# Decoder layer on one core: the result rows of the expert stage are stored by GpSimd, one indexed scatter per batch, in place of one plain transfer per four batches from SyncE

## The chip, the cores and the metric

The kernel runs on one core of a Trainium2 chip. The metric is device time in microseconds (us), the median of the timed runs. The engines are named as in the profile: PE (TensorE), PEld (its weight loads), DVE (VectorE), ACT (ScalarE), POOL (GpSimd) and SP (SyncE); SPq is SP's queue, from which it issues DMAs.

## The reference

Input x has 64 batches of 128 tokens, 128 wide; ctx has 64 batches of 120. Three blocks follow each other, each ending in a layer norm over the sum with its input:

```
x = layernorm(x + linear_attention(x))                  # 16 heads of 8, softplus q and k, causal
x = layernorm(x + cross_attention(ctx, x))              # 16 heads of 64; queries from x, keys from ctx and x
x = layernorm(x + experts(x))                           # the output
```

The last block, in which the change lies:

```
scores  = softmax(x @ gate_w.T)                         # 8 experts
top 2 of them, weights normalised and times 2.5 -> combine[token, expert]
y       = sum_e combine[:, e] * (silu(x @ w_gate[e]) * (x @ w_up[e])) @ w_down[e]     # width 176 each
y      += silu(x @ sw_gate) * (x @ sw_up) @ sw_down     # shared expert, width 352
out     = (h - mean(h)) / sqrt(var(h) + 1e-5),  h = x + y
```

All of it is float32. The kernel gets float32 products from three passes of TensorE over operands split into a high and a low part.

## The kernel before

The three blocks run one after the other: `linear_attention`, `cross_attention` and `experts`. X, the layer's current value, stays in on-chip memory; token s of every batch lies on partition s. The order of the work on each engine is written out by hand: there is one instruction stream per engine, and semaphores tie the streams together.

`experts` works on groups of four batches, 512 tokens at once: 16 groups. The hidden width of the eight experts and the shared one, 1408 + 352 = 1760, is cut into 14 blocks of 128 (the last has 96); blocks 0 to 10 belong to the experts, 11 to 13 to the shared one. Step t of the pipeline works on three groups at once: it prepares group t (transposes, logits, routing), runs the 14 blocks of group t-1, and finishes group t-2 (normalises and stores).

In block n of a step:
- PE multiplies by gate and up, three matmuls each (`split_product`, L489 to L491), spreads the routing weights for an expert block (L1325), and adds block n-3 into `ps_y` (the down product), for which it waits until `hidden_lo` of that block is there. At the start of the next step it transposes the routing weights `c_rows` (L1347).
- ACT takes SiLU (L1172) and rounds the previous block's `hidden` to `hidden_hi` (L1161).
- DVE multiplies SiLU by up (L1257) and, for an expert block, by the routing weight (L1263). From block 8 on it also runs a share of the 20 small routing operations of group t (L1217 to L1240), the last four in block 13, behind that block's L1257. Its write of `hidden` in block n waits until POOL has finished `hidden_lo` of block n-2, since `hidden` has two buffers.
- POOL computes `hidden_lo = hidden - hidden_hi` of block n-1 (L1117, function `hidden_lo`). In block 4 it makes the reciprocal deviation of group t-2 (L1131, L1133); in blocks 5, 7, 9 and 11 it writes one batch's normalised rows into `result` (L1138), each behind that block's `hidden_lo`.
- SP waits for the four `result` rows of group t-2 and issues one 256 KB store (L1098). `result` has two buffers, `par` 0 and 1, and `stored[par]` counts landed stores.

At the start of `experts` POOL writes three constants (L1107 to L1110): `half`, the expert numbers `index`, for which DVE waits before it copies the first `x_rows`, and the zeroed `cT`.

Of the kernel before, what the change touches and what calls it, by code (L numbers as in the profile page):

```python
# [24 lines left out]
P = 128  # L25
EXPERTS = 8
B = 64
S = 128
# [6 lines left out]
def wait(engine, semaphore, count):  # L35

    if not isinstance(count, int) or count > 0:
        engine.wait_ge(semaphore, count)  # L38


def wait_apart(engine, opened, *waits):

    waits = [(semaphore, count if isinstance(count, int) else engine.to_reg(count)) for semaphore, count in waits]
    engine.wait_ge(opened, 1)
    for semaphore, count in waits:
        wait(engine, semaphore, count)


def pipelined(engine, step, count=B, head=4, tail=4):

    for t in range(count + tail):
        step(t, t % 2)


def there(s, count=B):

    return not isinstance(s, int) or 0 <= s < count


def landed(s, parity):

    return (s - parity) * 8 + 16
# [943 lines left out]
GROUP = 4  # L1010
TOKENS = GROUP * S
GROUPS = B // GROUP
# [3 lines left out]
def experts(nc, X, ident, later, out):  # L1016
# [19 lines left out]
    with ExitStack() as stack:  # L1036
        room = Room(nc, stack, "e")
# [24 lines left out]
        result = room.sbuf("result", [P, 2, GROUP, D])  # L1062
# [7 lines left out]
        half_ready = room.sem("half_ready")  # L1070
# [10 lines left out]
        sum_ready, stat_ready, mom_ready = room.sem("sum_ready"), room.sem("stat_ready"), room.sem("mom_ready")  # L1081
        vare_ready, rstd_ready, result_ready = room.sem("vare_ready"), room.sem("rstd_ready"), room.sem("result_ready")
        stored = [room.sem(f"stored{n}") for n in range(2)]
        block = stack.enter_context(nc.Block())

        def run(engine, step):
            pipelined(engine, step, GROUPS, 2, 2)

        def here(s):
            return there(s, GROUPS)  # L1090

        @block.sync
        def _(sp):
            def step(t, par):
                s2 = t - 2
                if here(s2):
                    sp.wait_ge(result_ready, (s2 + 1) * GROUP)
                    sp.dma_start(out[bass.ds(s2 * GROUP, GROUP)].rearrange("b s d -> s b d"), result[:, par]  # L1098
                                 ).then_inc(stored[par], 16)

            run(sp, step)
            for par in range(2):
                sp.wait_ge(stored[par], GROUPS // 2 * 16)

        @block.gpsimd
        def _(pool):
            nc.gpsimd.memset(half[:], -0.5).then_inc(half_ready, 1)  # L1107
            for e in range(EXPERTS):
                nc.gpsimd.memset(index[:, e:e + 1], float(e)).then_inc(index_ready, 1)
            nc.gpsimd.memset(cT[:].bitcast(F32), 0.0).then_inc(zero_ready, 1)  # L1110
            pool.wait_ge(half_ready, 1)

            def hidden_lo(s, n):

                rows = rows_of[n]
                pool.wait_ge(hidden_hi_ready, s * NB + n + 1)
                nc.gpsimd.tensor_tensor(hidden_part[1][0:rows, n % RING, :], hidden[0:rows, n % 2, :],  # L1117
                                        hidden_part[0][0:rows, n % RING, :].bitcast(F32), ALU.subtract
                                        ).then_inc(hidden_lo_ready, 1)

            def step(t, par):
                s1, s2 = t - 1, t - 2
                for n in range(NB):
                    if n == 0 and here(s2):
                        hidden_lo(s2, NB - 1)
                    if n and here(s1):
                        hidden_lo(s1, n - 1)
                    if n == 4 and here(s2):

                        wait_apart(pool, half_ready, (mom_ready, (s2 + 1) * GROUP))  # L1130
                        nc.gpsimd.tensor_scalar(vare[:], mom[:, :, 1], EPS, None, ALU.add).then_inc(vare_ready, 1)  # L1131
                        pool.wait_ge(vare_ready, s2 + 1)
                        nc.gpsimd.tensor_tensor(rstd[:], vare[:], half[:], ALU.pow).then_inc(rstd_ready, 1)  # L1133
                    if n in (5, 7, 9, 11) and here(s2):
                        k = (n - 5) // 2

                        wait_apart(pool, half_ready, (rstd_ready, s2 + 1), (stored[par], landed(s2, par) - 16))
                        nc.gpsimd.tensor_scalar(result[:, par, k, :], hsum[:, k, :], mom[:, k, 0:1], rstd[:, k:k + 1],  # L1138
                                                ALU.subtract, ALU.mult).then_inc(result_ready, 1)

            run(pool, step)

        @block.scalar
# [239 lines left out]
def decoder(nc, x, ctx, Wq, bq, Wk, bk, Wv, bv, Wo, bo, m_g, m_b, l_g, l_b, xWq, xWkv, xWout,  # L1383
            gate_w, w_gate, w_up, w_down, sw_gate, sw_up, sw_down, out):
    lat = nc.dram_tensor("latents", (B, S, D), F32, kind="Internal").ap()
    with ExitStack() as stack:
        X = stack.enter_context(nc.sbuf_tensor("X", [P, B * D], F32))
        ident = stack.enter_context(nc.sbuf_tensor("ident", [P, P], F32))
        tri = stack.enter_context(nc.sbuf_tensor("tri", [P, P], F32))
        later = LaterWeights(nc, stack, (m_g, m_b, l_g, l_b), xWq, xWkv, xWout, gate_w, w_gate, w_up, w_down, sw_gate,  # L1390
                             sw_up, sw_down)
        constants(nc, ident, tri)
        linear_attention(nc, X, lat, ident, tri, x, (Wq, Wk, Wv, Wo), (bq, bk, bv, bo), later)
        cross_attention(nc, X, lat, ctx, ident, later)
        experts(nc, X, ident, later, out)
# [23 lines left out]
```

## Time and profile before

| | us |
|---|---|
| median of 3 runs | 2271.53 (2271.13 to 2274.04) |
| the profiled execution, its own time | 2267.62 |
| its span, first to last instruction | 2265.6 |
| granted TensorE clock, mean over the span | 0.985 of full speed |
| busy: PE, DVE, ACT, POOL | 2163.8, 1575.9, 1479.8, 1386.0 |

The span is that of one execution; it was taken 3.9 us under the median of the timed runs. `experts` fills it from 1697 us on. Each instruction has a line of the kernel, an engine and the names of the tiles it writes and reads; `out<-in` is the order. In brackets behind an instruction stands how long its engine had been idle and who ended that. The DMAs of the result appear as instructions of SPq, with the issue's own duration and, apart from it, the time to landing.

### The profile page before, as it was taken

Reading aid. Unit: us, or ns where it says so; the run is one execution under the profiler, and the core shown is the slowest. Engines: PE = TensorE matmul, PEld = TensorE weight load, DVE = VectorE, ACT = ScalarE, POOL = GpSimd, SP = SyncE. Lnnn points to the kernel's source line nnn. Section 1 sums busy time; section 2 is a strip of 40 time slices with the busy share of each in tenths; the row PEclk is TensorE's granted clock in tenths of the full one; section 3 lists DMA queues with packets and bytes.
Section 4 is the critical chain, followed back from the end, with each engine's and each line's share of the span. In section 5 each row is a group of like instructions: output and inputs, shape, how many; then the busy total and the mean of one; then the engine's idle time right before and its main releaser. Section 6 shows DMA issues by size and latency. Waiting matters only on the chain. (4 is left out here: it accounts for less than half of the span.)

```text
span 2265.6 us, 44642 instructions
## 1 busy us (share of the span) xinstructions
PE 2163.8 (96%) x16233; PEld 1841.5 (81%) x16233; DVE 1575.9 (70%) x3455; ACT 1479.8 (65%) x3820; POOL 1386.0 (61%) x1481
## 2 busy tenths in 40 slices
PE   6899967999999999999999999999989999999998
PEld 3455547999999999999999999999977777777776
DVE  3899965666666666666666666666657777777775
ACT  4788845667676666666676766666655665665664
POOL 4788856566565565565665655655654666666666
PEclk9999979999999999999999999999999999999999
DMA  3311110000000000000000000000000000000000
GB/s 93 113 33 33 30 30 5 6 10 6 10 7 6 10 6 6 11 6 6 11 6 10 7 6 10 6 6 10 6 1 1 10 5 10 10 5 10 10 5 14
DMA packets 52794, 33.46 MB, mean 15 GB/s; under 512 B 2968, under 2 KB 50274, under 8 KB 52450
## 3 DMA queue, kind: packets, MB, share of 16 engines
q1 hardware_dynamic: 50174, 26.30, 4.0%
q10 hardware_dynamic: 2404, 4.33, 0.7%
q8 instruction: 131, 2.15, 0.4%
q14 instruction: 85, 0.70, 0.1%
HBM read 22.22 MB, written 8.39 MB: 14 GB/s over the span
## 5 line engine op out<-in xcount | busy, mean ns | idle before, releaser
L653 POOL TENSOR_TENSOR x_prob<-x_prob,x_inv 128x496 f32<-128x496 f32 x514 | 521.7, 1015 | 546.9 <-DVE x_inv L792 546.9
L728 ACT ACTIVATE x_prob<-x_ps_S,x_nmax 128x248 f32<-128x248 f32 x1028 | 473.2, 468 | 130.4 <-DVE x_nmax L786 130.3
L786 DVE TENSOR_REDUCE x_nmax<-x_ps_S 128x2 f32<-128x496 f32 x515 | 345.5, 671 | 181.3 <-PE x_ps_S L491 181.1
L736 ACT COPY x_probT<-x_ps_T 124x512 f32<-124x512 f32 x512 | 300.7, 587 | 225.0 <-PE x_ps_T L955 225.0
L1117 POOL TENSOR_TENSOR e_hidden_lo<-e_hidden,e_hidden_hi 128x512 fp32r<-128x512 f32 x224 | 291.8, 1306 | 196.6 <-ACT e_hidden_hi L1161 195.7
L489 PE MATMUL x_ps_S<-x_kT_lo,x_G_hi 128*128 128x248 f32 x1030 | 329.6, 320 | 0.0
L955 PE MATMUL x_ps_T<-ident,x_prob 128*124 128x128 f32 x2048 | 315.1, 276 | 11.3 <-POOL x_prob L653 11.3
L955 PEld LDWEIGHTS x_ps_T<-ident,x_prob 128*124 128x124 f32 x2048 | 237.8, 139 | 71.7 <-POOL x_prob L653 29.2
L490 PE MATMUL x_ps_S<-x_kT_hi,x_G_lo 128*128 128x248 f32 x1030 | 287.3, 279 | 0.0
L491 PE MATMUL x_ps_S<-x_kT_hi,x_G_hi 128*128 128x248 f32 x1030 | 286.7, 278 | 0.0
L772 DVE TENSOR_TENSOR x_G_lo<-x_ps_G,x_G_hi 128x512 fp32r<-128x512 f32 x259 | 178.8, 690 | 129.2 <-ACT x_G_hi L722 129.1
L930 PE MATMUL x_ps_O<-x_probT,x_V 124*64 124x128 f32 x4096 | 251.8, 276 | 0.2 <-ACT x_probT L736 0.2
L930 PEld LDWEIGHTS x_ps_O<-x_probT,x_V 124*64 124x64 f32 x4096 | 220.9, 137 | 18.9 <-issue 5.1
L1172 ACT ACTIVATE e_silu<-e_ps_gate 128x512 f32<-128x512 f32 x224 | 134.5, 601 | 154.5 <-PE e_ps_gate L491 149.0
L722 ACT CAST x_G_hi<-x_ps_G 128x512 fp32r<-128x512 f32 x259 | 152.0, 587 | 91.6 <-PE x_ps_G L491 91.4
L728 ACT ACTIVATION_READ_ACCUMULATOR x_prob<-x_ps_S,x_nmax 128x1 f32 x1028 | 206.8, 201 | 0.0
L490 PEld LDWEIGHTS x_ps_S<-x_kT_hi,x_G_lo 128*128 128x128 f32 x1030 | 196.3, 191 | 0.0
L489 PEld LDWEIGHTS x_ps_S<-x_kT_lo,x_G_hi 128*128 128x128 f32 x1030 | 195.4, 190 | 0.0
L491 PEld LDWEIGHTS x_ps_S<-x_kT_hi,x_G_hi 128*128 128x128 f32 x1030 | 194.8, 189 | 0.0
L1257 DVE TENSOR_TENSOR e_act_up<-e_silu,e_ps_up 128x512 f32<-128x512 f32 x176 | 120.3, 684 | 90.2 <-PE e_ps_up L491 52.8
L778 DVE COPY x_V<-x_ps_V 124x512 f32<-124x512 f32 x259 | 176.6, 682 | 1.8 <-PE x_ps_V L491 1.8
L1161 ACT CAST e_hidden_hi<-e_hidden 128x512 fp32r<-128x512 f32 x224 | 137.4, 613 | 26.7 <-DVE e_hidden L1263 25.9
(199 smaller groups left out, 5135.3 us busy)
## 6 DMA issues: line engine op xcount, KB each, us to landing
x_nk<-latents SPq DMA_DIRECT2D x34, 124.0 KB
lin_x_rows<-in_x SPq DMA_DIRECT2D x32, 128.0 KB, 2.4
latents<-lin_nlat SPq DMA_DIRECT2D x32, 128.0 KB, 1.8
out_dram<-e_result SPq DMA_DIRECT2D x16, 256.0 KB, 2.2
x_nk<-in_ctx SPq DMA_DIRECT2D x34, 120.0 KB, 2.1
w_wkv<-in_L_xattn_Wkv SPq DMA_DIRECT2D x1, 1024.0 KB, 6.1
w_rows<-in_L_ffn_w_gate SPq DMA_DIRECT2D x1, 704.0 KB, 5.8
w_rows<-in_L_ffn_w_up SPq DMA_DIRECT2D x1, 704.0 KB, 6.2
```

The source lines that it names most:

```text
L489: nc.tensor.matmul(out, stationary[0], moving[1], start=first, stop=False)
L490: nc.tensor.matmul(out, stationary[1], moving[0], start=False, stop=False)
L491: return nc.tensor.matmul(out, stationary[0], moving[0], start=False, stop=last)
L653: nc.gpsimd.tensor_tensor(prob[:, k], prob[:, k], inv[:, k].unsqueeze(2).broadcast_to([P, 2, K]), ALU.mult).then_inc(prob_ready, 1)
L728: nc.scalar.activation(prob[:, k, h, :], ps_S[:, n % BANKS, h * K:(h + 1) * K], ACT.Exp, bias=nmax[:, k, h:h + 1], accum_out=total[:, k, h ...
L736: nc.scalar.copy(probT[0:KT, s % (2 * GANG)], ps_T[0:KT, s % 2, :]).then_inc(probT_ready, 1)
L772: nc.vector.tensor_tensor(G_part[1][:, pair].rearrange("p h u q -> p (h u q)"), ps_G[:], G_part[0][:, pair].bitcast(F32).rearrange("p h u ...
L778: nc.vector.tensor_copy(V[:, hf, u, tile, :], ps_V[0:KT, :]).then_inc(V_ready, 1)
L786: nc.vector.tensor_reduce(nmax[:, k, :], ps_S[:, n % BANKS, 0:2 * K].rearrange("p (h k) -> p h k", h=2), AX, ALU.max, negate=True).then_in ...
L930: last = nc.tensor.matmul(ps_O[h * DH:(h + 1) * DH, k * S:(k + 1) * S], V[:, j // 4, u, tile, (j % 4 * 2 + h) * DH:(j % 4 * 2 + h + 1) * D ...
L955: last = nc.tensor.transpose(ps_T[0:KT, s % 2, at:at + S], prob[:, s % RINGS, h, tile * KT:(tile + 1) * KT], ident[:])
L1117: nc.gpsimd.tensor_tensor(hidden_part[1][0:rows, n % RING, :], hidden[0:rows, n % 2, :], hidden_part[0][0:rows, n % RING, :].bitcast(F32), ...
```

## The change

POOL stores each batch's rows itself, right behind the operation that wrote them. It makes a table of row numbers once (`row_index[s, b] = 128 b + s`, an iota), and each store is a scatter: partition s of `result` goes to row `row_index[s, b]` of the output seen as 8192 rows of 128 floats, 512 bytes a row, 128 rows or 64 KB an instruction. There are 64 such stores of 64 KB where there were 16 of 256 KB. SP issues nothing in this block any more and waits at its end for 8 x 4 stores per buffer. Before a store POOL waits on its own semaphore `result_ready` until the rows have been written. The wait on `stored[par]` ahead of each `result` counts in units of a batch now and means the same: that the group two before has landed. The wait on `half_ready` ahead of it is gone.

```diff
+        row_index = room.sbuf("row_index", [P, B], mybir.dt.uint32)
+        rows_ready = room.sem("rows_ready")
+        rows_out = out.rearrange("b s d -> (b s) d")
...
         @block.sync
         def _(sp):
-            def step(t, par):
-                s2 = t - 2
-                if here(s2):
-                    sp.wait_ge(result_ready, (s2 + 1) * GROUP)
-                    sp.dma_start(out[bass.ds(s2 * GROUP, GROUP)].rearrange("b s d -> s b d"), result[:, par]
-                                 ).then_inc(stored[par], 16)
-
-            run(sp, step)
             for par in range(2):
-                sp.wait_ge(stored[par], GROUPS // 2 * 16)
+                sp.wait_ge(stored[par], GROUPS // 2 * 16 * GROUP)
...
             nc.gpsimd.memset(half[:], -0.5).then_inc(half_ready, 1)
+            nc.gpsimd.iota(row_index[:], [[S, B]], base=0, channel_multiplier=1).then_inc(rows_ready, 1)
+            pool.wait_ge(rows_ready, 1)
...
-                        wait_apart(pool, half_ready, (rstd_ready, s2 + 1), (stored[par], landed(s2, par) - 16))
+                        wait(pool, rstd_ready, s2 + 1)
+                        wait(pool, stored[par], (s2 - par) // 2 * GROUP * 16)
                         nc.gpsimd.tensor_scalar(result[:, par, k, :], hsum[:, k, :], mom[:, k, 0:1], rstd[:, k:k + 1],
                                                 ALU.subtract, ALU.mult).then_inc(result_ready, 1)
+                        pool.wait_ge(result_ready, s2 * GROUP + k + 1)
+                        row = s2 * GROUP + k
+                        nc.gpsimd.indirect_dma_start(rows_out, bass.IndirectOffsetOnAxis(row_index[:, row:row + 1], 0),
+                                                     result[:, par, k, :], None).then_inc(stored[par], 16)
```

On POOL, in a step that finishes a group, this stood between the deviation and the end of the block for the third batch (`e_` marks the tiles of `experts`; the semaphores waited for stand in brackets):

```order
L1131 TENSOR_SCALAR e_vare<-e_mom 128x4 [waits e_mom_ready,e_half_ready]
L1133 TENSOR_TENSOR e_rstd<-e_vare,e_half 128x4 [waits e_vare_ready]
L1117 TENSOR_TENSOR e_hidden_lo<-e_hidden,e_hidden_hi 128x512 [waits e_hidden_hi_ready]
L1138 TENSOR_SCALAR e_result<-e_hsum,e_mom,e_rstd 128x128 [waits e_rstd_ready,e_half_ready]
L1117 TENSOR_TENSOR e_hidden_lo<-e_hidden,e_hidden_hi 128x512 [waits e_hidden_hi_ready] x2
L1138 TENSOR_SCALAR e_result<-e_hsum,e_mom,e_rstd 128x128 [waits e_rstd_ready,e_half_ready]
L1117 TENSOR_TENSOR e_hidden_lo<-e_hidden,e_hidden_hi 128x512 [waits e_hidden_hi_ready] x2
L1138 TENSOR_SCALAR e_result<-e_hsum,e_mom,e_rstd 128x128 [waits e_rstd_ready,e_half_ready]
```

And this stands there now, the same stretch of POOL (line numbers of the changed file):

```order
L1128 TENSOR_SCALAR e_vare<-e_mom 128x4 [waits e_mom_ready,e_half_ready]
L1130 TENSOR_TENSOR e_rstd<-e_vare,e_half 128x4 [waits e_vare_ready]
L1114 TENSOR_TENSOR e_hidden_lo<-e_hidden,e_hidden_hi 128x512 [waits e_hidden_hi_ready]
L1136 TENSOR_SCALAR e_result<-e_hsum,e_mom,e_rstd 128x128 [waits e_rstd_ready]
L1140 DMA out_dram<-e_result,e_row_index 8192x128 [waits e_result_ready]
L1114 TENSOR_TENSOR e_hidden_lo<-e_hidden,e_hidden_hi 128x512 [waits e_hidden_hi_ready] x2
L1136 TENSOR_SCALAR e_result<-e_hsum,e_mom,e_rstd 128x128 [waits e_rstd_ready]
L1140 DMA out_dram<-e_result,e_row_index 8192x128 [waits e_result_ready]
L1114 TENSOR_TENSOR e_hidden_lo<-e_hidden,e_hidden_hi 128x512 [waits e_hidden_hi_ready] x2
L1136 TENSOR_SCALAR e_result<-e_hsum,e_mom,e_rstd 128x128 [waits e_rstd_ready]
L1140 DMA out_dram<-e_result,e_row_index 8192x128 [waits e_result_ready]
```

Four stores a step have moved into POOL's stream, each between a `result` and the next `hidden_lo`. At the start of the block POOL now has one more instruction, and the first `index` waits for it:

```order
L1102 MEMSET e_half 128x4
L1103 IOTA e_row_index 128x64
L1106 MEMSET e_index 128x1 [waits e_rows_ready]
L1106 MEMSET e_index 128x1 x7
L1107 MEMSET e_cT 128x1024
```

Before, the eight writes of `index` stood right behind that of `half`. PE, DVE and ACT keep their instructions and their order.

## Rows read from the trace of the kernel before

**Rows 1.** The page: busy time and share of the span of each engine.
```profile
PE 2163.8 (96%) x16233; PEld 1841.5 (81%) x16233; DVE 1575.9 (70%) x3455; ACT 1479.8 (65%) x3820; POOL 1386.0 (61%) x1481
```
**Rows 2.** One step by window: window, length, busy PE, PEld, DVE, ACT, POOL, clock.
```profile
2097.70:2131.96 34.26, 34.26 (x157) 27.09 (x156) 26.11 (x59) 20.81 (x35) 22.64 (x21) 1.00 0.03 9
```
**Rows 3.** Timeline of POOL, blocks 7 to 13: start, us, what, idle before.
```profile
2105.55 0.80 POOL L1138 TENSOR_SCALAR e_result<-e_hsum,e_mom,e_rstd 128x128 f32<-128x128 f32 x1
2106.30 2.56 POOL L1117 TENSOR_TENSOR e_hidden_lo<-e_hidden,e_hidden_hi 128x512 fp32r<-128x512 f32 x2
...
2113.96 1.29 POOL L1117 TENSOR_TENSOR e_hidden_lo<-e_hidden,e_hidden_hi 128x512 fp32r<-128x512 f32 x1
2116.03 1.30 POOL L1117 TENSOR_TENSOR e_hidden_lo<-e_hidden,e_hidden_hi 128x512 fp32r<-128x512 f32 x1 [0.78 <-ACT e_hidden_hi L1161]
```
**Rows 4.** Timeline of DVE in block 13 of the same step.
```profile
2115.59 0.68 DVE L1257 TENSOR_TENSOR e_hidden<-e_silu,e_ps_up 96x512 f32<-96x512 f32 x1
2116.20 1.17 DVE L1236 TENSOR_TENSOR e_picked<-e_both,e_score 128x32 f32<-128x32 f32 x1
...
2117.85 0.19 DVE L1240 TENSOR_TENSOR e_c_rows<-e_both,e_c_rows 128x32 fp32r<-128x32 f32 x1
```
**Rows 5.** Groups by line of DVE, 1770 to 2230 us: count, busy us, mean ns.
```profile
L1236 DVE TENSOR_TENSOR e_picked<-e_both,e_score 128x32 f32<-128x32 f32 x14 | 16.4, 1174 | 0.0
...
L1235 DVE TENSOR_TENSOR e_both<-e_first,e_second 128x32 f32<-128x32 f32 x14 | 2.7, 192 | 0.5
```
**Rows 6.** Timeline of PE: the first transposes of the next step.
```profile
2118.11 0.60 PE L1347 MATMUL e_ps_m<-ident,e_c_rows 128*16 128x128 f32 x4
```
**Rows 7.** Groups of POOL by shape: count, busy us, mean ns, idle before.
```profile
L283 POOL TENSOR_TENSOR lin_kv<-lin_qk,lin_v 128x1024 f32<-128x1024 f32 x64 | 135.2, 2133 | 3.2 <-POOL lin_v L275 0.8
...
L1133 POOL TENSOR_TENSOR e_rstd<-e_vare,e_half 128x4 f32<-128x4 f32 x16 | 16.6, 1039 | 1.3
...
L1109 POOL MEMSET e_index<- 128x1 f32 x8 | 0.3, 99 | 0.0
L98 POOL TENSOR_SCALAR_AFFINE_SELECT ident<-ident 128x128 f32<-128x128 f32 x1 | 0.3, 293 | 0.2 <-POOL tri L96 0.2
```
**Rows 8.** DMA issues, KB each, median us to landing; the tile of the result.
```profile
lin_w_rows<-in_L_attn_Wq SPq DMA_DIRECT2D x1, 64.0 KB, 1.9
...
L1098 SPq DMA_DIRECT2D out_dram<-e_result x16: 372/372/403, 1771.4 to 2263.0; - x16
DMA to landing us min/median/max: 2.2/2.2/2.8
```
**Rows 9.** Timeline of POOL and PE in the last two steps.
```profile
2239.24 0.79 POOL L1138 TENSOR_SCALAR e_result<-e_hsum,e_mom,e_rstd 128x128 f32<-128x128 f32 x1
...
2251.38 2.53 POOL L1117 TENSOR_TENSOR e_hidden_lo<-e_hidden,e_hidden_hi 128x512 fp32r<-128x512 f32 x2 [0.78 <-ACT e_hidden_hi L1161]
...
2253.97 0.50 PE L489 MATMUL e_ps_y<-e_hidden_lo,e_down_hi 96*128 96x512 f32 x1 [0.28 <-POOL e_hidden_lo L1117]
...
2259.87 3.13 POOL L1138 TENSOR_SCALAR e_result<-e_hsum,e_mom,e_rstd 128x128 f32<-128x128 f32 x4 [0.17 <-POOL e_rstd L1133]
```
**Rows 10.** Timeline at the start of the expert stage.
```profile
1697.68 0.95 POOL L1110 MEMSET e_cT<- 128x1024 f32 x1
...
1697.98 0.93 DVE L1249 COPY e_x_rows<-X 128x512 f32<-128x512 f32 x1
...
1699.06 1.09 PE L1366 MATMUL e_ps_m<-ident,e_x_rows 128*128 128x128 f32 x4 [1.40 <-DVE e_x_rows L1249]
```
**Rows 11.** PE after idle times in cross attention; a window behind each, columns as above.
```profile
341.82 0.49 PE L489 MATMUL x_ps_V<-x_wv_lo,x_kT_hi 128*124 128x512 f32 x1 [1.30 <-DVE x_V L778]
349.16 1.11 PE L955 MATMUL x_ps_T<-ident,x_prob 128*124 128x128 f32 x4 [3.61 <-POOL x_prob L653]
...
349.10:352.40 3.30, 3.24 (x15) 3.25 (x16) 0.74 (x2) 1.09 (x4) 3.22 (x3) 0.51 0.00 0
341.80:344.00 2.20, 2.18 (x16) 2.04 (x17) 1.18 (x2) 0.00 (x0) 2.13 (x2) 1.00 0.00 0
```

## The prediction, made before the changed kernel ran

> **What bounds the kernel now.** The page comes first: PE is busy for 96% of the span, POOL for 61% [rows 1]. The change touches only the expert stage, so one of its steps is read next, as a window. A step takes 34.26 us and PE is busy in all of it, at the full clock (1.00); POOL is busy for 22.64 us and so idle for 11.62 us [rows 2]. By the shares the four added stores a step would have room. But idle time is of use only where POOL isn't waited for, so the timelines of the three engines at one place come next. They show a chain that has almost no slack.
>
> POOL, from its second `result` of the step (start 2105.55) to the end of `hidden_lo` of block 12 (2116.03 + 1.30 = 2117.33), has 11.78 us [rows 3]. In it lie three `result` of 0.8 us and six `hidden_lo` of 1.3 us, 10.2 us of work; 1.58 us are idle. DVE's block 13 depends on it twice. Its L1257 may write `hidden` only when `hidden_lo` of block 11 is done (2113.96 + 1.29 = 2115.25; L1257 starts at 2115.59), and the operation behind it, `picked`, takes 1.17 us, from 2116.20 to 2117.37, which is when POOL's `hidden_lo` of block 12 ends [rows 3, 4]. That this is no accident shows in the groups: all 14 `picked` of the steady stage take 1174 ns on average, while the sum `both` of the same shape takes 192 ns [rows 5]. A DVE operation on two on-chip inputs stands still while POOL runs a two-input operation. Behind `picked` come three more, and `c_rows` is there at 2117.85 + 0.19 = 2118.04 [rows 4]. PE transposes it from 2118.11 [rows 6], in its turn and 0.07 us later. So whatever makes POOL's `hidden_lo` of block 12 end later than 2117.33 makes PE wait, and PE has no idle time in which to win it back.
>
> **The change part by part.** Let x be what one store adds to POOL's stream: g, the wait on POOL's own semaphore before it, plus d, the time for which POOL writes the 128 descriptors.
>
> g: POOL waited for itself once before, ahead of the last `result` group; the row has 0.17 us idle there [rows 9]. I take 0.15.
>
> d: no row shows a DMA issued by POOL. From below, the cheapest POOL instruction at all takes 0.10 us and SP's issue of the whole 256 KB store 0.37 us [rows 7, 8]. From above, POOL's work on 128 x 1024 elements takes 2.13 us [rows 7]. Between these I go by the row it is most like, a small tile handled by a slow piece of code per element: `rstd`, 4 elements a partition, 1.04 us [rows 7]. A scatter must read an index and form an address for each of 128 rows, a little more than that, so d = 1.2 and x = 1.35.
>
> On what a DMA issued by GpSimd costs, the Trainium skill (DMA: Bandwidth & Descriptors, Latency and other measured facts) puts the first byte about 1 us after the issue, for the descriptors that software writes. With d = 1.0 instead of 1.2 the same sum would come to about 2302. No row here shows it.
>
> In the steady steps, three stores lie in the stretch above (the first, ahead of 2105.55, falls into POOL's pause around the ACT table loads and costs nothing). The stretch then takes 10.2 + 3x where it had 11.78, as its pauses fill first: PE waits 3x - 1.58 = 4.05 - 1.58 = 2.47 us at `c_rows`. That happens where a step both finishes one group and routes another, steps 2 to 15: 14 x 2.47 = 34.6 us. All that hangs behind is moved alike; the other place where PE might wait, `hidden_lo` of block 11 for the down product, comes earlier in the chain and is less late.
>
> In step 16 there is no routing, and PE waits for POOL's `hidden_lo` themselves; the last begins at once when block 12's ends [rows 9]. From the second `result` (2239.24) POOL has 3 x 0.8 + 7 x 1.3 + 3x = 11.5 + 4.05 = 15.55 us and ends at 2254.8 in place of 2253.9: 0.9 us.
>
> The tail: four `result` take 3.13 us from 2259.87 [rows 9]. With three stores between them and one behind, the last store's descriptors are written at 2259.87 + 3.13 + 4 x 1.35 = 2268.4. A 64 KB DMA lands 1.9 us after its issue, of which 0.37 is the issue itself [rows 8]: 2269.9. Before, SP issued at 2263.0 and the rows landed 2.2 us later, at 2265.2 [rows 8]. That adds 4.7 us.
>
> The start: the iota stands ahead of the eight `index` writes and of `cT`. DVE's first copy, 1697.98 to 1698.91, outlasts the write of `cT` (to 1698.63) by little, and PE follows it at 1699.06 [rows 10], so the iota is on the path. It fills 64 columns; POOL's generated pattern of 128 columns took 0.29 us [rows 7]. With its wait, 0.4 us.
>
> By the Trainium skill (GPSIMD Engine Reference, Instruction dispatch) the first call of a freshly loaded GpSimd routine pays about 6 us; if the iota did, the sum would be some 5.6 us more. No row shows such a pause at a first POOL operation of this kernel.
>
> What goes: SP's 16 issues were on no engine's path but the last one, counted above. The wait on `stored` is always long met, a store having a whole step of 34 us and more to land. The DMA engines are at 3% in a step [rows 2], so 512-byte pieces cost nothing there.
>
> Sum: 34.6 + 0.9 + 4.7 + 0.4 = 40.6 us, on the profiled execution 2267.62 + 40.6 = 2308.2. The median of the runs lies 3.9 us above that execution, so 2271.53 + 40.6 = 2312 us. With x from 1.15 to 1.5 (d 1.0 to 1.35) it is 2302 to 2319.
>
> **The rivals.**
>
> Covered stores (the other side: not slower). If POOL only hands the store on, as SP does, and works on while the descriptors are written, d is near POOL's cheapest instruction, 0.10 us. Then 3x = 0.75 us, under the 1.58 us of idle time, and PE never waits. What is left is the tail, 2259.87 + 3.13 + 4 x 0.25 + 1.53 = 2265.5, 0.3 us more, and the iota's 0.4: 2272 us. It decides while x is below 1.58 / 3 = 0.53 us. For it speaks POOL's 11.6 us of idle time a step; against it, that POOL has no second unit that shows up in any row.
>
> Cheap stores. With d = 0.6, x = 0.75: 0.67 us a step, 9 us in all, tail and start 2.7: 2284. The DVE operations on two inputs may fall upon `hidden_lo` more often when POOL is late, at 0.9 to 1.0 us each, so up to 2296. I put it at 2290.
>
> Dear stores. DVE is busy for 26.11 of 34.26 us [rows 2], and rows 4 and 5 show the two engines excluding each other. If the writing of descriptors is held up by DVE in the same way, or reads its indices one by one, d goes to the 2.13 us of the costliest regular POOL operation: x = 2.28, 14 x 5.26 = 73.6 us, step 16 3.7, the tail 8.4, start 0.4: 86 us, 2358 us. Against it: only a `hidden_lo`, not `result` (one on-chip tile), has been seen to hold up DVE, and DVE's large operations read PSUM with one input.
>
> Of just this the Trainium skill warns (SBUF — State Buffer, the "DVE blocks DMA" trap): GpSimd can't write descriptors while DVE runs certain copies between SBUF tiles, and a DMA of 0.62 us took 3.1 us. By that rule the exposed operation here is the copy of `x_rows`, which lies after the stores of a step, so it would cost nothing; where the rule held for more of DVE's operations, the sum with 3.1 us would be near 2400. The rows agree with the exclusion between POOL's and DVE's operations (1174 against 192 ns); no row shows it for descriptors.
>
> The clock. PE has no pause in a step now. After 1.30 us of idle time the granted clock was 1.00, after 3.61 us it was 0.51 for 3.3 us, the level of 1.2 GHz for 2.4 [rows 11]. A wait of 2.47 us lies between. If each wait drops the clock, 3.3 x 0.49 = 1.6 us more are lost in each of 14 steps, 22.6 us: 2335 us.
>
> **How the numbers follow.** The forecast (PE waits 1.9 to 2.9 us a step, clock kept) 0.45; dear stores 0.15; the clock 0.12; cheap stores 0.15; covered stores 0.13. A measurement of this kernel can tell a change of about 0.2%, 4.5 us, from none. Only covered stores stay within that; faster would need the smaller last transfer to outweigh all else, 0.02. So slower 0.87, same 0.11, faster 0.02. The range goes from 2284, the formula's value for cheap stores, to 2358, dear stores at the upper bound; covered stores and a d above 2.13 us are left out. The forecast's own range is 2302 to 2319.
>
> **What would show it.** In the trace of the changed kernel: POOL's stream with a gap or a DMA of 1.0 to 1.35 us behind each `result`; in a steady step PE idle for about 2.5 us before the transposes of `c_rows`, released by DVE, 14 times, and nowhere else; a step of 36.7 us; `picked` still near 1.1 us; the clock at 1.00 in a step; 7 to 8 us from the last step's first `result` to the last store. The forecast is wrong if PE stays busy throughout a step (stores covered), if its waits come at `hidden_lo` first, if POOL's `hidden_lo` or `result` themselves are longer, or if the clock in a step falls below 1.00.

## The result, and the profile after

| | before | after |
|---|---|---|
| median, us (range, runs) | 2272.78 (2271.13 to 2274.05, 4) | 2323.28 (2322.0 to 2329.49, 4) |
| ratio, 95% interval | | 1.0228 [1.0208, 1.0248] |
| profiled execution, its span | 2267.62, 2265.6 | 2329.49, 2327.4 |
| expert stage in it, first memset to end | 568.3 | 624.2 |

Slower by 50.5 us, where 40.6 was forecast. The two profiled executions stand 5.8 us apart before the expert stage begins (1697.4 and 1703.2 us). The experiments' kernels, unchanged there, began it between 1697.4 and 1702.2 as well, so that part varies by itself. The terms are therefore compared inside the stage: +55.9 us, of which the start is 0.24, steps 2 to 15 are 14 x 3.27 = 45.8, step 16 is 1.44 and the tail 8.4. (The tail is what lies behind the last `rstd`: the last four `result`, their stores and the end of the block.) The medians show less than the stage does. The other three executions after ran 6.0 to 7.5 us shorter than the profiled one, the four before 3.5 to 6.4 us longer. By estimate, then, most began the stage early after the change and late before it; no trace of them is at hand. One of the four executions of the memset experiment below took 5482.39 us, for a reason that is not on record, while the other three took 2322.1 to 2322.4.

The page of the kernel after, busy times, against [rows 1]; then one step as a window, columns as in [rows 2].

```profile
PE 2180.4 (94%) x16233; PEld 1842.1 (79%) x16233; DVE 1600.2 (69%) x3455; ACT 1481.4 (64%) x3820; POOL 1453.0 (62%) x1546
```
```profile
2122.47:2160.00 37.53, 35.05 (x156) 26.86 (x156) 27.86 (x60) 21.03 (x35) 26.90 (x24) 1.00 0.02 8
```

PE's clock stays at full speed and PE now idles 2.48 us a step (37.53 less 35.05); the other 0.8 us of the longer step are in longer spans of the matmuls beside the waits, whose ends are modelled. The tile of the result, in place of [rows 8]: each store occupies POOL for 1.08 us.

```profile
L1140 POOL DMA_INDIRECT out_dram<-e_result,e_row_index x64: 1045/1077/1229, 1763.2 to 2320.8; - x64
...
DMA to landing us min/median/max: 2.3/2.3/3.2
```

The timeline of POOL, blocks 9 to 13, against [rows 3]:

```profile
2149.00 0.79 POOL L1136 TENSOR_SCALAR e_result<-e_hsum,e_mom,e_rstd 128x128 f32<-128x128 f32 x1
2150.07 1.08 POOL L1140 DMA_INDIRECT out_dram<-e_result,e_row_index  x1 [0.28 <-POOL e_result L1136]
2151.19 2.54 POOL L1114 TENSOR_TENSOR e_hidden_lo<-e_hidden,e_hidden_hi 128x512 fp32r<-128x512 f32 x2
2153.71 0.79 POOL L1136 TENSOR_SCALAR e_result<-e_hsum,e_mom,e_rstd 128x128 f32<-128x128 f32 x1
2154.78 1.06 POOL L1140 DMA_INDIRECT out_dram<-e_result,e_row_index  x1 [0.28 <-POOL e_result L1136]
2155.89 2.54 POOL L1114 TENSOR_TENSOR e_hidden_lo<-e_hidden,e_hidden_hi 128x512 fp32r<-128x512 f32 x2
```

From `result`'s start to the next `hidden_lo` it takes 2.19 us here (2151.19 less 2149.00), 2.18 on the mean of the three in the stretch. Before, the same three took 0.76, 0.88 and 0.81 us, 0.82 on the mean; the one that rows 3 show is the shortest. So a store adds 1.37 us. The stretch from the second `result` (2144.30) to the end of `hidden_lo` of block 12 (2158.43) is 14.13 us in place of 11.78, so that end comes 2.35 us late. DVE in the same place, against [rows 4]:

```profile
2150.78 3.01 DVE L1227 SCALAR_TENSOR_TENSOR e_rest<-e_first,e_score 128x32 f32<-128x32 f32 x1
...
2155.84 2.65 DVE L1236 TENSOR_TENSOR e_second<-e_order,e_col 128x32 f32<-128x32 f32 x1
2158.52 0.19 DVE L1237 TENSOR_TENSOR e_both<-e_first,e_second 128x32 f32<-128x32 f32 x1
2158.63 0.68 DVE L1259 TENSOR_TENSOR e_hidden<-e_silu,e_ps_up 96x512 f32<-96x512 f32 x1
2159.24 0.18 DVE L1238 TENSOR_TENSOR e_picked<-e_both,e_score 128x32 f32<-128x32 f32 x1
...
2159.89 0.19 DVE L1242 TENSOR_TENSOR e_c_rows<-e_both,e_c_rows 128x32 fp32r<-128x32 f32 x1
```

The operation held until that `hidden_lo` ends is no longer `picked` (0.18 us now) but `second`, two routing operations earlier. All that was done before now stands behind it, block 13's `hidden` included, and `c_rows` follows the `hidden_lo` by 1.65 us (2158.43 to 2160.08) in place of 0.71. The sum is 2.35 + 0.94 = 3.29, which is the step's 3.27 within the reading. PE's three waits of a step:

```profile
2152.54 0.50 PE L489 MATMUL e_ps_y<-e_hidden_lo,e_down_hi 128*128 128x512 f32 x1 [0.26 <-POOL e_hidden_lo L1114]
...
2154.96 0.48 PE L489 MATMUL e_ps_up<-e_xT_lo,w_up_hi 128*96 128x512 f32 x1 [0.76 <-DVE e_hidden L1259]
...
2160.14 0.60 PE L1349 MATMUL e_ps_m<-ident,e_c_rows 128*16 128x128 f32 x4 [1.46 <-DVE e_c_rows L1242]
```

The last stores of the run, then the wait of SyncE at the block's end (how often, longest us), which was 0.2 before:

```profile
2319.72 0.79 POOL L1136 TENSOR_SCALAR e_result<-e_hsum,e_mom,e_rstd 128x128 f32<-128x128 f32 x1
2320.79 1.05 POOL L1140 DMA_INDIRECT out_dram<-e_result,e_row_index  x1 [0.28 <-POOL e_result L1136]
```
```profile
SPq L1036 <- PEq L1036: 4.0, 1, 4.0
```

What SyncE waits for is GpSimd's own closing instruction, a DRAIN. It began at 2320.6 us, ahead of the last store, and ended at 2327.14, 5.30 us behind that store's end (duration in ns, start in us):

```profile
L1036 POOLq DRAIN x1: 6588/6588/6588, 2320.6 to 2320.6; - x1
```

### The profile page after: what moved, and what is told of

Its sections match the earlier page's. It is cut to its first block and busy times, and to the rows that moved or that the text cites. A ratio compares the mean times of both kernels' runs of the same rounds, so it can differ in the third digit from the quotient of the medians.

```text
span 2327.4 us, 44683 instructions
## 1 busy us (share of the span) xinstructions
PE 2180.4 (94%) x16233; PEld 1842.1 (79%) x16233; DVE 1600.2 (69%) x3455; ACT 1481.4 (64%) x3820; POOL 1453.0 (62%) x1546
```

## The experiments

Each is an edit of the kernel after, timed against the kernel before in the same job. Its stage start varies as said, so steps (from one `rstd` to the next) and ends are read from the traces.

**Smaller stores by SyncE**, and no iota.
```diff
+                    for k in range(GROUP):
+                        sp.wait_ge(result_ready, s2 * GROUP + k + 1)
+                        sp.dma_start(out[s2 * GROUP + k], result[:, par, k, :]).then_inc(stored[par], 16)
-                        nc.gpsimd.indirect_dma_start(rows_out, bass.IndirectOffsetOnAxis(row_index[:, row:row + 1], 0),
-                                                     result[:, par, k, :], None).then_inc(stored[par], 16)
```


> One store per batch (64 of 64 KB), but issued by SyncE; GpSimd has no store and no iota. Theory (GpSimd's occupancy costs, not the number or size of the stores): as before within 1 us, about 2272, PE without a pause in a step of 34.26 us, tail at most 0.5 us shorter. Rival (64 KB pieces of 512-byte rows, or the finer counting of semaphores, cost something by themselves): a good part of the 50 us shows here too, over 2280.


2267.31 us, ratio 0.9992 [0.998, 1.0003]; step 34.26, as the theory had it. The 64 transfers in place of 16 cost nothing; all of the loss comes from who issues them and where.

**GpSimd stores without indices**, and no iota.
```diff
-                        nc.gpsimd.indirect_dma_start(rows_out, ..., result[:, par, k, :], None)
+                        nc.gpsimd.dma_start(out[row], result[:, par, k, :])
```


> The changed kernel with a plain DMA of the same 64 KB from GpSimd's queue in place of the indexed one, and no iota. Theory (what costs is that GpSimd writes 128 descriptors in software): duration near the 1.08 us of the indexed store, a step of 37.2 to 37.6 us, 2315 to 2324 us. Rival (the index makes it dear): the plain store takes 0.4 us or less, x falls to about 0.7 and the time to about 2285.


2305.88 us, 1.0153 [1.0131, 1.0175]; step 36.19. The store takes 0.60 us in place of 1.08, the wait ahead of it 0.29, as in the kernel after. Both expectations missed, the measured step lies between them. The indices cost 1.34 of the 3.27 us a step; 1.93 remain.

**The same stores in POOL's pauses** of the next step; those of the last group stay where they were.
```diff
+            STORE_AT = (0, 2, 3, 6)
+                    if n in STORE_AT and here(t - 3) and t - 3 < GROUPS - 1:
+                        store(t - 3, 1 - par, STORE_AT.index(n))
```


> The same 64 indexed stores on GpSimd, but those of a group (all but the last) are issued one step later, behind hidden_lo in blocks 0, 2, 3 and 6, where GpSimd had pauses of 2.3, 1.0, 1.5 and 2.7 us. Theory (the stores cost only because they lie between block 7 and block 12, where GpSimd has 1.58 us of pauses): a step of 34.3 to 34.5 us, PE without a pause at c_rows; what stays is the tail, 8.5 us, and the iota: 2280 to 2285 us. Rival (a scatter costs wherever it stands, by holding up VectorE or through its descriptors): a step of 35.5 us or more, over 2298.


2281.06 us, 1.0043 [1.003, 1.0056]. Its step as a window:

```profile
2098.00:2132.26 34.26, 34.26 (x158) 27.10 (x157) 26.12 (x59) 20.82 (x36) 26.76 (x24) 1.00 0.02 9
```

POOL does the same work a step as in the kernel after (26.76 against 26.90 us) and it costs nothing. Not the load but the place made the 45.8 us. What is left is the tail, as the theory had it.

**A filler in place of the stores**, 128 x 1168 elements in 1.07 us; SyncE stores per batch, without iota.
```diff
+                        pool.wait_ge(result_ready, s2 * GROUP + k + 1)
+                        nc.gpsimd.memset(filler[:], 0.0).then_inc(filled, 1)
```


> The stores are issued by SyncE per batch; on GpSimd, in the place of each store, behind the same wait for result_ready, stands a memset of 128 x 1168 elements of unused memory, about 1.08 us. Theory (GpSimd's time alone moves the chain): a step of 37.2 to 37.6 us as with the stores; the tail some 3 us shorter than with them; 2314 to 2321. Rival (writing descriptors holds up VectorE's two-input operations in a way of its own, and a memset doesn't): the step stays at about 36.9 us, 2.6 us over 34.26, and the time near 2310.


2322.39 us, 1.0225 [1.0198, 1.0253]. The median is the one that the theory gave, but not by its mechanism. The steps are of two kinds, 36.86 and 38.4 us, and the first is the rival's 36.9. `rest`, issued during the memset, takes 0.18 us: a memset does not hold it. In its place the cast of `c_rows` is held, 1.29 us by block 13's `hidden_lo`, and PE's wait is nearly in one piece. After it the clock falls to the level of 1.2 GHz in 6 of 14 steps, at 1.57 us a time. The window shown is 0.50 up to 2125.0 and back at full speed within it, 0.65 on the mean:

```profile
2122.04 0.67 PE L1355 MATMUL e_ps_m<-ident,e_c_rows 128*16 128x128 f32 x4 [1.91 <-DVE e_c_rows L1248]
```
```profile
2123.30:2127.00 3.70, 3.70 (x15) 2.90 (x13) 1.21 (x2) 1.11 (x3) 0.00 (x0) 0.65 0.00 0
```

**`rest` with one input.** It tests whether the two inputs of the DVE operation are what gets it held; the choice of the second expert is not the reference's.
```diff
-v.scalar_tensor_tensor(rest[:], first[:], -4.0, score[:], ALU.mult, ALU.add)
+v.tensor_scalar(rest[:], score[:], -4.0, 1.0, ALU.mult, ALU.add)
```


> The changed kernel; VectorE's routing operation rest is computed from one tile in place of two (the top-2 choice is therefore not the reference's, the amount of work is). Theory (rest, held for 3.0 us through the store and two hidden_lo, makes VectorE arrive at the end of hidden_lo of block 12 with six operations still to do in place of four): VectorE goes through second in the gap before the last store, only picked is held, c_rows comes 0.7 us after hidden_lo of block 12 as in the kernel before, the wait for VectorE before up of block 13 goes; a step of 36.6 us in place of 37.53, 13 us in all, about 2310. Rival (VectorE's holds lie beside GpSimd's own delay and cost nothing): step unchanged at 37.5 us, 2323.


2327.86 us, 1.0247 [1.023, 1.0264]; step 37.53, unchanged, and:

```profile
2149.09 3.00 DVE L1227 TENSOR_SCALAR e_rest<-e_score 128x32 f32<-128x32 f32 x1
```

The idea fell. This operation (`tensor_scalar`) is held with one input too. Not every one is: a `TENSOR_REDUCE` takes 0.17 to 0.19 us in these kernels, beside a store or a `hidden_lo` too.

**Each store one block later**, behind the next `hidden_lo`, its rows long ready.
```diff
+                    if n in (6, 8, 10, 12) and here(s2):
+                        k = (n - 6) // 2
+                        row = s2 * GROUP + k
+                        pool.wait_ge(result_ready, row + 1)
+                        nc.gpsimd.indirect_dma_start(...)
```


> The changed kernel with each indexed store issued one block later, behind the next hidden_lo, so that its rows have long been written and no two hidden_lo stand together. Theory: GpSimd's wait before a store falls from 0.28 to 0.17 us, three times 0.11 less on the chain, and VectorE gets in between single hidden_lo, which takes away up to 0.9 us: a step of 36.3 to 37.2 us, 2305 to 2319. Rival (only the sum of GpSimd's work counts and the wait isn't reducible): step 37.5 us, 2323.


2370.99 us, 1.0426 [1.0402, 1.0451]; step 39.9 at first and 40.96 later, 48 us slower than the kernel after, so both expectations were wrong. The last store now stands right ahead of the last two `hidden_lo`, and `picked` itself is held through all three; the clock then falls in every step (0.92 over one). Block 12's `hidden_lo` is 2.91 us late and `c_rows` follows it by 1.94, which makes 38.40 us a step; the rest, up to 2.56, is the clock:

```profile
2145.54 1.07 POOL L1135 DMA_INDIRECT out_dram<-e_result,e_row_index  x1 [0.17 <-issue]
2146.65 2.48 POOL L1114 TENSOR_TENSOR e_hidden_lo<-e_hidden,e_hidden_hi 128x512 fp32r<-128x512 f32 x2
```
```profile
2146.18 3.01 DVE L1240 TENSOR_TENSOR e_picked<-e_both,e_score 128x32 f32<-128x32 f32 x1
```
```profile
2149.91 1.02 PE L1351 MATMUL e_ps_m<-ident,e_c_rows 128*16 128x128 f32 x4 [3.48 <-DVE e_c_rows L1244]
```

**Routing one block earlier**, blocks 8 to 12.
```diff
-                    if ROUTE_AT <= n and here(t):
+                    if ROUTE_AT <= n < NB - 1 and here(t):
-                        blocks = NB - ROUTE_AT
+                        blocks = NB - 1 - ROUTE_AT
```


> The changed kernel with VectorE's 20 routing operations spread over blocks 8 to 12 in place of 8 to 13, so that c_rows is ready a block earlier and doesn't hang behind hidden_lo of block 12. Theory (the place where the stores hurt is the c_rows chain; without it only hidden_lo of block 11 is late for TensorE's down product, by about 1.1 us): no wait at c_rows, a step of 35.3 to 35.9 us, 2294 to 2302. Rival (TensorE is slowed by GpSimd's lateness wherever it shows, the other waits grow by what this one loses): a step of 37.2 us or more, 2318 or more.


2316.71 us, 1.0194 [1.0177, 1.0211]; step 36.70, between the two expectations. `picked` is again what is held to the end of block 12's `hidden_lo`, `c_rows` follows it by 0.73 us, and the 2.42 us by which that `hidden_lo` is late stay. It cures the second part of the loss alone.

**A filler with two inputs**, an addition of 128 x 424 elements; it took 0.90 us, not the 1.08 meant.
```diff
-                        nc.gpsimd.memset(filler[:], 0.0).then_inc(filled, 1)
+                        nc.gpsimd.tensor_tensor(filler[:, 0], filler[:, 1], filler[:, 1], ALU.add).then_inc(filled, 1)
```


> SyncE stores per batch; in the place of each of GpSimd's stores stands an addition of two on-chip inputs over 128 x 424 elements, of about 1.08 us, which nothing reads. Theory A (a small DVE operation begun during a GpSimd instruction that shares its way into the on-chip memory is held until GpSimd has its next pause, so through the two hidden_lo behind it too, and a store counts as such an instruction): rest is held for about 3 us as with the stores, picked or second as there, the step 37.5 us, the median 2318 to 2330. Theory B (only a store's descriptor writing makes the hold last over three instructions; a two-input operation holds DVE to its own end, like hidden_lo before): rest is held for 1 us or less, the chain at the step's end is that of the filler without inputs, step 36.8 to 38.4 with the clock falling in some steps.


2304.26 us, 1.0155 [1.014, 1.017]; step 36.40. `rest` begins with the first of two `hidden_lo` and is let go at its end, not at that of the second. `col`, a reduction, passes, and `equal` is held by the second:

```profile
2137.67 1.32 DVE L1235 SCALAR_TENSOR_TENSOR e_rest<-e_first,e_score 128x32 f32<-128x32 f32 x1
2139.03 0.19 DVE L1236 TENSOR_REDUCE e_col<-e_rest 128x4 f32<-128x32 f32 x1
2139.25 0.99 DVE L1238 TENSOR_TENSOR e_equal<-e_rest,e_col 128x32 f32<-128x32 f32 x1
```

Against a rest held for 3 us, theory A fell. Its 1.32 us is above B's "1 us or less" too, and the step is below B's 36.8 (the filler was shorter). That the long holds appear only in kernels with stores on GpSimd is what B said.

The steps of five kernels by the two parts, against before: by how much block 12's `hidden_lo` ends late, and how far `c_rows` comes behind it.

| kernel | added to POOL a time | late | `c_rows` behind | sum | step |
|---|---|---|---|---|---|
| before | | | 0.71 | | 34.26 |
| plain store | 0.98 | 1.22 | 1.41 | 36.18 | 36.19 |
| two-input filler | 0.92 | 1.04 | 1.82 | 36.41 | 36.40 |
| memset | 1.08 | 1.50 | 1.81 | 36.86 | 36.86 |
| after | 1.37 | 2.35 | 1.65 | 37.55 | 37.53 |
| after, routing early | 1.39 | 2.42 | 0.73 | 36.70 | 36.70 |

(The memset's row is that of its steps at full clock.) In all five rows the lateness is three times what was added, less 1.7 us: that was the slack of the stretch. The second part, 0.7 to 1.1 us, came with every addition, store or not, and went when DVE's order moved.

**The tail**, in four kernels. First only group 0 by GpSimd, the rest by SyncE per batch:

> GpSimd stores only the first group of four batches by index; SyncE stores the other 15 groups per batch. Theory (the 3.4 us more between the last landed store and the end of the span come from having used GpSimd's DMA queue at all, a fixed price at the end of the block): steps of 34.26 us but for the first, 3.3 us longer; the span ends 4 to 6 us after the last result where it ends 2.6 us after it without GpSimd stores; about 2277. Rival (the late end comes from the last stores landing late): the end is as in the kernel before, 2.6 us after the last result, about 2274.


```diff
+                        if s2 == 0:
+                            pool.wait_ge(result_ready, s2 * GROUP + k + 1)
+                            nc.gpsimd.indirect_dma_start(...)
```
2274.2 us, 1.001 [1.0001, 1.002]; all steps 34.26 but the first, 37.57. GpSimd is not late at its end, so the price is not one that any store brings. Then the stores in POOL's pauses again, with the last group by SyncE:
```diff
+                sp.wait_ge(result_ready, (GROUPS - 1) * GROUP + k + 1)
+                sp.dma_start(out[(GROUPS - 1) * GROUP + k], result[:, 1, k, :]).then_inc(last_stored, 16)
```


> GpSimd's indexed stores of a group in its pauses of the next step (blocks 0, 2, 3 and 6), as in the kernel with the stores in the pauses, but the last group's four batches are stored by SyncE, one transfer each. Theory (the stores cost time only where they stand in the chain of hidden_lo, and at the end only because the last rows leave through GpSimd's queue): the step is 34.26 us, the span ends about 2 us after the last result as it does with SyncE's stores, what is left is the iota's 0.3 us: the median within 0.2% of before, ratio 0.999 to 1.002. Rival (the four stores of the last group but one, which now stand in the last step between its hidden_lo, rstd and first result, delay that step or land late): the end 3 to 5 us later than before, ratio 1.0015 to 1.0025.


2275.47 us, 1.0024 [1.0014, 1.0034]. Its stage begins at 1697.4 us like that of before, and its span ends 4.2 us later, as the rival had it: 0.3 is the iota with its wait, 1.3 group 14's last store, which stands between the last results, and 2.6 a late end, though SyncE issued the last stores. Then the last two groups by SyncE:

```diff
-                    if n in STORE_AT and here(t - 3) and t - 3 < GROUPS - 1:
+                    if n in STORE_AT and here(t - 3) and t - 3 < GROUPS - 2:
```


> As the kernel before it (GpSimd's indexed stores in its pauses of the next step), but the last two groups are stored by SyncE, so that GpSimd's last store lies some 30 us ahead of the end and none stands between its last results. With the last group alone by SyncE the span came to 2269.8 us: the last result ended 1.6 us later than before (the iota's 0.3 us and one store of 1.3 us among the last results), and the block's end took 5.2 us from GpSimd's last instruction where it takes 2.0 us with SyncE's stores. Theory (GpSimd is late at the block's end only if it issued a store in the last few microseconds): both go, the span ends 2.0 us after the last result, near 2265.5 us where the part ahead of the block takes the time it took before, ratio 0.9985 to 1.001. Rival (its end is late once it has issued many stores, however long ago: four at the start of the block were not enough): the end stays 5.2 us behind its last instruction, span near 2268.5 us, ratio 1.001 to 1.0025.


2272.97 us, 1.0008 [0.9998, 1.0019]. The late end stays: the theory of the last few microseconds fell. Last, group 13 alone by GpSimd:

```diff
+                    if n in STORE_AT and t - 3 == ONE_GROUP:
+                        store(t - 3, 1 - par, STORE_AT.index(n))
```


> SyncE stores per batch; only the four batches of group 13 are stored by GpSimd, in its pauses of the next step, the last of them some 30 us ahead of the end. Fifty-six stores of which the last lay 26 us ahead of the end left GpSimd's end 4.9 us behind its last instruction; four stores 500 us ahead of the end did not (2.0 us). If what counts is how long ago the last store was, the span ends 4.5 to 5.5 us after the last result, as with the fifty-six; if it is how many there were, 2.0 us after it. The steps take 34.26 us by both; the median 2269 to 2275 us by the first, 2266 to 2272 by the second, which the time alone can hardly tell apart: the trace's end is what is asked.


2270.96 us, 0.9995 [0.9985, 1.0005]. Their ends:

| kernel | stores by GpSimd | last one begins before the span's end, us | span's end behind GpSimd's last work, us | end of its DRAIN behind the same, us |
|---|---|---|---|---|
| SyncE per batch | 0 | | 2.0 | 0.07 |
| group 0 | 4 | 495 | 2.0 | 0.42 |
| group 13 | 4 | 28 | 2.0 | 0.42 |
| all but two groups | 56 | 31 | 4.9 | 4.67 |
| all but the last group | 60 | 9 | 5.2 | 4.99 |
| in the pauses | 64 | 7 | 5.5 | 5.30 |
| after | 64 | 7 | 5.5 | 5.30 |

With 4 stores, early or late, the span pays nothing; with 56 it pays 31 us after the last of them. So it is not the last stores that make the end late, as I had written, but having issued many. The last column shows how that sets in. GpSimd's DRAIN ends 0.08 us later for each store that GpSimd has issued: (0.42 - 0.07) / 4 = 0.09, (4.67 - 0.07) / 56 = 0.08, (5.30 - 0.07) / 64 = 0.08. With 0 or 4 stores it ends before SyncE's last store has landed, and that landing sets the 2.0 us. The lines of group 13 and of all but two groups:

```profile
L1036 POOLq DRAIN x1: 3233/3233/3233, 2261.9 to 2261.9; - x1
L1036 POOLq DRAIN x1: 7560/7560/7560, 2265.4 to 2265.4; - x1
```

Counts between 4 and 56 were not run, and what the DRAIN does in that time no row shows.

## Why the prediction was right, and where its terms were off

The time came into the range, and the cause is the one given: POOL itself is occupied by each store, in a chain with little slack. It is above the forecast's own range of 2302 to 2319, though, and lies in the wide one that the rivals had opened. What one store adds was met: 1.37 us against x = 1.35. That took some luck, since d was 1.08 us (forecast 1.2) and g 0.28 (0.15), two errors that cancel. The forecast took d from a row of `rstd`; the Trainium skill (DMA: Bandwidth & Descriptors, Latency and other measured facts) speaks of about 1 us for the first byte, and 1.08 us at GpSimd with 2.3 to landing agrees in size.

- **Steps 2 to 15**, 34.6 forecast, 45.8 measured: the term that was most mis-sized. The part for `hidden_lo` was 2.47 a step and came to 2.35, since the slack was 1.7 us and not 1.58. The step that failed is "behind `picked` come three more": it took the order of holds before as fixed, whereas a late POOL makes `second` the held operation and moves block 13's `hidden` behind it, 0.94 us. The routing-early kernel takes just that away.
- **Where PE waits.** Forecast at `c_rows` and nowhere else; there are two more waits, 0.26 and 0.76 us of idle time, ahead of it, and the first is for `hidden_lo`, which the forecast had named as a sign of being wrong. The three come to 2.48 us, so that the 2.47 forecast for one wait was met by coincidence: the step grew by 3.27. "Nowhere else" was wrong.
- **Clock.** It stayed at 1.00, as the forecast had it. One idle time of 1.62 us a step left it there too (two-input filler); one of 1.9 us was followed by the low level in 6 of 14 steps (memset), and one of 3.46 to 3.51 in all 14 of the alternate kernel's. The forecast's own single wait of 2.47 us lies between these. Its price for a fall, 1.6 us, was right: 1.57. That the splitting into three pieces saved the clock is a reading of these rows; no run isolates it.
- **Tail**, 4.7 forecast, 8.4 measured. The stores took the time given for them, 8.72 us from the first `result` to the last store's end against 8.53. Missing was the DRAIN: the span ended 5.5 us behind the last store, where the forecast's sum leaves 1.9.
- **Step 16**, 0.9 forecast, 1.44 measured. The stretch from the second `result` gave 0.99, 15.66 us in place of 14.67. The other 0.45 belongs to the step's first store, which the sum left out: the pause that it fills there was only 1.00 us long. **Start**, 0.4 forecast, 0.24 measured; the iota took 0.19 us and the first store 1.23. The 6 us for a first call (the Trainium skill, GPSIMD Engine Reference, Instruction dispatch) are seen at neither.
- **Covered and cheap stores** fell with d. **Dear stores** too: no descriptor writing was stretched, 1045 to 1229 ns over 64. The trap of the Trainium skill (SBUF — State Buffer, "DVE blocks DMA") does not show, but the copy of `x_rows`, which by that rule would be the one to stretch a store, never began during one here. What the rows show is the other order, DVE's operations being held while GpSimd stores.

## What to carry to other kernels

A store issued by GpSimd is an instruction of GpSimd's stream: price it at 1.1 us (0.6 without indices) plus 0.3 for its wait, and read from the timeline, not from the busy share, whether the place has that much slack. The same four stores a step cost 45.8 us in one place and nothing in another. At the end of the block add 0.08 us for each store that GpSimd has issued, as far as nothing else ends later. When an engine in such a chain is made later, ask again which operation of its neighbour is held, and what queues behind that one.

## What the runs showed of the hardware

- A small DVE operation between on-chip tiles passes while GpSimd writes an indexed store's descriptors, in 0.15 to 0.20 us, if it begins up to 0.34 us into the store. If it begins 0.63 to 1.07 us into it, it is held to the end of the second `hidden_lo` behind: 3.00 to 3.05 us from 0.63 to 0.70, and 2.63 to 2.71 from 1.00 on, over the steps of four kernels (after, one-input `rest`, routing early, alternate). Reductions, a reciprocal at 0.97 us and the statistics of `e_stat` are not held. Behind a plain store `rest`, which begins with the pair, is held for 2.58 us.
- Without a store, a hold lasts 1.0 to 1.3 us, to the end of one `hidden_lo`, and a memset does not hold DVE. Why it lasts through the second one behind a store is open; a `tensor_scalar` with one input is held as long as the operation with two.
- GpSimd's closing DRAIN ends 0.07 us behind its last work without stores, 0.42 after 4 stores and 4.67 to 5.30 after 56 to 64, about 0.08 us a store.
- GpSimd idles 0.28 us between `result` and its store when it must wait for itself, 0.16 to 0.17 when the rows have long been there.
- No version beat the kernel before: the best with many stores on GpSimd (all but two groups, in the pauses) is equal to it, 1.0008 [0.9998, 1.0019].
